# A state-space scan loop: the gates and convolution taps between the scans and the product with C

## The reference

```
xz = hidden_states @ in_proj_w.T;  x, z = split(xz)          # 1024 channels each
x = silu(causal_conv4(x) + conv_b)
dt, Bm, Cm = split(x @ x_proj_w.T)                           # 128, 16, 16
dt = softplus(dt @ dt_proj_w.T + 2 * dt_proj_b)
deltaA = exp(dt[..., None] * A);  deltaB_u = dt[..., None] * Bm[:, :, None, :] * x[..., None]
states[t] = deltaA[t] * states[t-1] + deltaB_u[t]            # 1024 channels x 16 states
y = (sum(states * Cm, -1) + x * D) * z
out = y @ out_proj_w.T
```

## Time and profile before

| | us |
|---|---|
| median of 3 runs | 3632.25 |
| lowest and highest | 3627.57, 3633.32 |
| the profiled execution | 3633.67 |
| its span, first to last instruction | 3631.7 |

### The profile page before, as it was taken

How to read it: one execution, slowest core, us unless ns; L and a number is a source line. 1 busy time by engine, 2 the same in 40 slices (tenths; PEclk the granted TensorE clock), 3 DMA queues, 4 the chain that set the end, 5 groups by cost and what they waited for, 6 DMA issues and landing times.

```text
span 3631.7 us, 30799 instructions
## 1 busy us (share of the span) xinstructions
PE 2781.9 (77%) x10802; PEld 1660.2 (46%) x10802; DVE 2316.8 (64%) x2273; ACT 1223.6 (34%) x1640; POOL 1003.3 (28%) x500
## 2 busy tenths in 40 slices
PE   5888706888598989995647768786886767779997
PEld 2333605666246779993312223232332323366665
DVE  3564365666565556663559999899899997532221
ACT  3333000000212126562244543644454332423333
POOL 0000703333102100003025555455454553011111
PEclk8888858999798999997779989998998999889998
DMA  4333911000513426663125444443453455100000
GB/s 172 101 118 64 80 20 31 0 0 0 173 58 102 163 92 248 240 223 110 36 67 151 120 121 134 130 133 112 126 143 106 127 155 178 78 1 12 12 0 23
DMA packets 230910, 359.45 MB, mean 99 GB/s; under 512 B 88432, under 2 KB 106864, under 8 KB 225168
## 3 DMA queue, kind: packets, MB, share of 16 engines
q1 hardware_dynamic: 224816, 328.67, 32.6%
q0 software_dynamic: 5120, 16.78, 1.4%
q10 hardware_dynamic: 864, 12.58, 0.8%
HBM read 304.26 MB, written 65.27 MB: 102 GB/s over the span
## 4 chain that ended last, share of the span: by engine, by line
PE 44%; DVE 27%; issue 15%; ACT 6%; DMA 3%; POOL 2%; SPq 1%; another core or an unknown queue 0%; PEld 0%; PEldq 0%; DVEq 0%; POOLq 0%; ACTq 0%
DVE arena L1093 12%; DVE arena L1100 5%; PE psum L1946 4%; PE psum L1566 3%; PE psum L1567 3%; PE psum L2050 2%; PE psum L2044 2%; DVE tmpA L1885 2%; PE psum L1329 2%; PE psum L1331 2%; PE psum L1330 2%; PE psum L2077 2%; PE psum L1554 1%; PE psum L1555 1%; PE psum L393 1%
## 5 line engine op out<-in xcount | busy, mean ns | idle before, releaser
L587 POOL TENSOR_TENSOR arena<-arena 128x1024 f32<-128x1024 f32 x256 | 630.3, 2463 | 712.6 <-DVE arena L1100 390.0
L1464 PE MATMUL psum<-arena,cst 128*128 128x512 f32 x1024 | 550.2, 668 | 291.3 <-DVE arena L1100 257.8
L1093 DVE TENSOR_TENSOR_SCAN arena<-psum,arena 128x512 f32<-128x512 f32 x512 | 595.8, 1203 | 32.3 <-POOL arena L587 22.1
L764 ACT ACTIVATE psum<-arena,negA 128x512 f32<-128x512 f32 x512 | 351.3, 690 | 646.5 <-DVE arena L1093 646.2
L1464 PEld LDWEIGHTS psum<-arena,cst 128*128 128x128 f32 x1024 | 194.1, 205 | 633.3 <-DVE arena L1100 397.1
L1647 POOL TENSOR_TENSOR arena<-arena,cst 128x1024 f32<-128x1024 f32 x96 | 200.0, 2098 | 689.3 <-DMA v_tok<-arena 353.4
L1100 DVE TENSOR_TENSOR arena<-arena 128x1024 f32<-128x1024 f32 x256 | 370.2, 1447 | 0.0
L1409 PE MATMUL psum<-arena 128*128 128x512 f32 x512 | 238.5, 612 | 36.0 <-DVE arena L1063 19.9
L1566 PE MATMUL psum<-r 128*128 128x512 f32 x512 | 209.0, 408 | 33.3 <-ACT arena L848 23.3
L1946 PE MATMUL psum<-arena 128*128 128x512 f32 x384 | 190.8, 654 | 49.2 <-DVE arena L1792 24.6
L1203 DVE TENSOR_TENSOR r<-arena,r 128x512 fp32r<-128x512 f32 x64 | 44.2, 692 | 266.9 <-ACT r L853 266.8
(11 more groups left out here) (271 smaller groups left out, 5336.8 us busy)
## 6 DMA issues: line engine op xcount, KB each, us to landing
arena<-bc_scr SPq DMA_DIRECT2D x256, 512.0 KB, 4.9
arena<-w_exp SPq DMA_DIRECT2D x23, 1408.0 KB, 6.0
arena<-in_inw SPq DMA_DIRECT2D x32, 512.0 KB, 4.6
arena<-in_gu SPq DMA_DIRECT2D x24, 512.0 KB
x_scr<-arena SPq DMA_DIRECT2D x23, 512.0 KB, 6.6
arena<-in_dn SPq DMA_DIRECT2D x23, 512.0 KB, 6.9
arena<-x_scr SPq DMA_DIRECT2D x23, 512.0 KB, 7.0
o_scr<-arena SPq DMA_DIRECT2D x23, 512.0 KB, 5.6
```

Source lines behind the costliest of these rows:

```text
L587: nc.gpsimd.tensor_tensor(dB[:, k % 4], du[:, j:j + 2], BC[:, k % RING, 0].unsqueeze(1).broadcast_to([P, 2, T]), ALU.mult).then_inc(s["db_ ...
L764: nc.scalar.activation(psum[:, 2 + t], dt[:, b % 2, j + t], ACT.Exp, scale=negA2[:, at:at + 1]).then_inc(s["da_ok"], 1)
L1093: v.tensor_tensor_scan(dB[:, k % 4, t], psum[:, 2 + t], dB[:, k % 4, t], 0.0, ALU.mult, ALU.add).then_inc(s["sc"], 1)
L1464: ins = mm(psum[:, t], ident, dB[:, k % 4, t], start=(n == 0), stop=(n == NS - 1))
```

## The change

Two calls on VectorE move from the end of a step into `scan`, between the two scans and `times_c`. The gates stay at their steps 5, 7, ... 19. The convolutions stand in step 23 + 2c instead of 21 + 2c, that is one odd step later. No instruction is added or removed, and the lists of the other four engines are the same as before.

```
--- before.py
+++ after.py
@@ -1091,6 +1091,10 @@
                 for t in range(2):
                     dve.wait_ge(s["da_ok"], 2 * k + t + 1)
                     v.tensor_tensor_scan(dB[:, k % 4, t], psum[:, 2 + t], dB[:, k % 4, t], 0.0, ALU.mult, ALU.add).then_inc(s["sc"], 1)
+                if i % 2 and b and 5 <= i < 5 + 2 * NDT:
+                    gate(b - 1, i // 2 - 2)
+                if i % 2 and b + 1 < B and 23 <= i < 23 + 2 * NDT:
+                    conv(b + 1, (i - 23) // 2)
                 if k:
                     times_c(k - 1)
 
@@ -1136,8 +1140,6 @@
                             softplus(b, 1)
                         if i == 8:
                             times_dt(b, 1)
-                        if i % 2 and 5 <= i < 5 + 2 * NDT:
-                            gate(b - 1, i // 2 - 2)
                         if i in (38, 42, 53, 56):
                             residual_tile(b - 1, (38, 42, 53, 56).index(i))
                     if b >= 2:
@@ -1146,8 +1148,6 @@
                         if i == 28:
                             scale_dve(dve, 2 * B + b - 2)
                     if nx:
-                        if i % 2 and 21 <= i < 21 + 2 * NDT:
-                            conv(nx, (i - 21) // 2)
                         if i == 58:
                             log1p_parts(nx, 0)
                         if i == 61:
```

## The result

| | before | after |
|---|---|---|
| median, us | 3628.61 (3623.58 to 3633.32, 6 runs) | 3694.06 (3689.67 to 3701.02, 6 runs) |
| ratio to before | 1 | 1.0183, 95% interval 1.0167 to 1.0199 |
| profiled execution, us | 3633.67, span 3631.7 | 3689.67, span 3686.7 |
| TensorE's mean granted clock | 0.895 | 0.889 |

What follows compares the result with a forecast made beforehand. VectorE was taken to bound the scan loop. The terms 23.4 + 23.7 + 15.1 - 1.1 - 4.6 + 5.5 = +62 us, added to 3632.25, gave 3694 us, with a range of 3657 to 3718 us.

Steps and rivals of the forecast that it cites:

- The chain: Convolution steps: late taps hold up x_tile, then sums, GpSimd, scans, next taps; a turn of 14.76 us, against 10.58 before.
- Turns: Rounds from one tile's taps to the next tile's: 12.50 us at full clock, 2.26 us more for TensorE's lower clock.
- By batch: Convolution stages, scans of step 21 to those of step 38: +23.4, +23.7 and +15.1 us in batches one to three.
- the variance matmuls: Third batch, LayerNorm matmuls ahead of x_tile(3): they fill TensorE's idle time, so that turn has no clock penalty, 12.50 us.
- the scaling: Third batch, step 28: VectorE's 3.34 + 2.29 us, which cost full time before, now lie in a turn's idle time.
- x_tile(0): Batches two and three: it waits for the last gate, now one product earlier; -1.1 us, and -4.6 in the third.
- The gates: Ahead of the product, first operation and other product meet GpSimd's end: +0.24 us each, 23 gates in the loop, +5.5.
- Costed at nothing: the loads: Row and weight loads on SP's queue: no cost; without cover, at most one landing, 4.9 us, nine times.
- a cost of the place ahead of the product: Rival set for the experiments: work ahead of the product with C delays GpSimd, sums and row loads; no chance given.
- a clock without a share: Rival set for the experiments: TensorE's lower clock adds nothing to the turns, 3694 us stays; no chance given.
- A kept clock: Rival: TensorE's clock is kept or returns at once, turns of 12.50 us; +25 us, 3658 us, 12%.
- one that stays low through all of x_tile: Rival: TensorE's clock stays low for the whole tile, +1.0 us on 17 turns; +79 us, 3711 us, 18%.

Runs made afterwards that it cites:

- a1: The kernel before with only the gates moved between the scans and the product with C; ratio to before 0.9993, loop 3.4 us shorter.
- d1: The changed kernel with x_tile(2) to x_tile(7) one step later in TensorE's list; ratio to before 0.9937, loop 20.6 us shorter.
- d3: d1 with the gates behind the product as before and x_tile(0) and x_tile(1) at steps 18 and 19; ratio to before 0.9918.
- e1: d3 with each row load issued ahead of the weight load of its step on SyncE; ratio to before 0.9906, loop 1144.3 us.
- a3: The kernel before with only the taps one odd step later, still behind the product with C; ratio to before 1.0271, loop +92.4 us.
- c1: The changed kernel with five extra matmuls, result unread, ahead of each x_tile(2) to x_tile(7) on TensorE; ratio to before 1.0097.

## Why the prediction was right

The time was forecast as 3694 and is 3694.06 us. That the two agree so closely is in part chance: the change costs 65.5 us where 62 were forecast, and the runs of before came out 3.6 us lower. By steps:

**The chain** was right in mechanism and size. Turns in the first batch: from 1956.39 to 2030.93, the ends of taps(0) and taps(5), five of them, 14.91 us each against 14.76. x_tile and the idle time ahead of it, the longest and the shortest of the 18 bursts in tiles 2 to 7:

```profile
2015.49 6.75 PE L1409 MATMUL psum<-arena 128*128 128x512 f32 x8 [5.40 <-DVE arena L1063]
...
2319.19 5.09 PE L1409 MATMUL psum<-arena 128*128 128x512 f32 x8 [5.40 <-DVE arena L1063]
```

The 18 last 5.09 to 6.75 us, mean 5.88, against 5.86 from nine bursts of other places. (A tenth, behind 28.59 us of idle time at the loop's start, had taken 6.63 and was not counted.)

**By batch**, S(21) to S(38). The first of these starts and ends, after, in the order of batches: 1944.69 and 2056.26, 2275.91 and 2388.33, 2612.75 and 2725.93. That is 111.6, 112.4 and 113.2 us against 87.11, 86.94 and 93.29: +24.5, +25.5 and +19.9, where +23.4, +23.7 and +15.1 were forecast.

**The third batch** holds the steps that failed. I had the variance matmuls keep the clock, and the scaling lie wholly in idle time. The rows say otherwise:

```profile
2633.85 3.60 PE L393 MATMUL psum<-tmpA,onesd 128*128 128x512 f32 x8
2639.41 5.40 PE L1409 MATMUL psum<-arena 128*128 128x512 f32 x8 [1.97 <-DVE arena L1063]
```

```profile
2658.39 3.35 DVE L370 RECIPROCAL dec<-dec 128x512 f32<-128x512 f32 x1
...
2661.77 2.29 DVE L375 TENSOR_TENSOR arena<-arena,dec 128x2048 f32<-128x2048 f32 x1
...
2662.51 6.04 POOL L587 TENSOR_TENSOR arena<-arena 128x1024 f32<-128x1024 f32 x2 [10.81 <-PE psum L1464]
...
2666.29 2.34 DVE L1093 TENSOR_TENSOR_SCAN arena<-psum,arena 128x512 f32<-128x512 f32 x2 [2.23 <-POOL arena L587]
```

The variance matmuls themselves ran at full speed, and after 1.97 us of idle time x_tile still took 5.40: the turn was 14.61 us, not 12.50. The trace of before had a warning of this outside, four matmuls that took 3.64 us behind 1.98 us of idle time, where others took 1.98 behind the same:

```profile
2428.50 1.98 PE L1464 MATMUL psum<-arena,cst 128*128 128x512 f32 x4 [1.98 <-DVE arena L1100]
...
2748.68 3.64 PE L1464 MATMUL psum<-arena,cst 128*128 128x512 f32 x4 [1.98 <-DVE arena L1100]
```

And GpSimd's two products took 6.04 us together instead of 4.64 beside L375; the scans began at 2666.29, 2.2 us after the scaling's end. That turn was 16.86 us, against 14.76: 1.4 us for the held GpSimd, and most of the rest for an x_tile of 6.62 us. The Trainium skill (SBUF — State Buffer, Who interferes with whom) has the two engines exclude each other there: L375 has two SBUF inputs and came first, and GpSimd's first product began 1.55 us before its end, about the 1.4 us that it lost. I had cited that rule for the gates and not applied it here.

**x_tile(0).** In the third batch S(21) waits for GpSimd no more, as forecast, and x_tile(0) took 3.67 us there. From S(38) of the batch before to S(21), the second batch took 219.65 us instead of 218.05 (+1.6) and the third 224.42 instead of 226.87 (-2.4). With a third of the gates' 5.5 us in each, forecast were +0.7 and -2.8 (the 2.96 and 1.77 us that stand beside the -4.6 make 4.73). In the second batch x_tile(0) took 1.24 us longer than the 5.21 of the earlier trace rows, though the idle time ahead of it was shorter, so the earlier gate gained nothing there:

```profile
2265.23 6.45 PE L1409 MATMUL psum<-arena 128*128 128x512 f32 x8 [4.69 <-issue]
```

**The gates** cost 0.18 us each at most, not 0.24: two in turn in the changed kernel,

```profile
2229.41 0.90 DVE L1111 SCALAR_TENSOR_TENSOR arena<-arena,cst 128x512 f32<-128x512 f32 x1
...
2237.94 0.90 DVE L1111 SCALAR_TENSOR_TENSOR arena<-arena,cst 128x512 f32<-128x512 f32 x1
```

are 8.53 us apart against 8.35 in the earlier trace rows. (The 1.43 us that the prediction calls a distance of starts are a row's length; such a product takes 1.35 from start to next start, 0.24 more than one alone.) The gate's first operation has grown from 0.74 to 0.90 us, but the two products are no longer than before, where I had one of them grow too. Over the loop this is under 4 us; in the fourth batch, S(0) to S(21) with eight gates and no x_tile, it is 0.7 (102.44 us against 101.74). In a1 it does not show against what x_tile(0) gains.

**Costed at nothing: the loads.** In the changed kernel this held; no wait for rows is in its list. In d1 and d3, where the turns are short again, the cover was gone, and e1 shows its price: 6.6 us in the convolution stages, 4.4 in the whole loop, all of it in longer products with C.

**The sum.** In the profiled loops the three stages cost 7.6 us more than forecast, and the rest of the loop came to -1.6 us where -0.2 was forecast: together +68.2, not +62. The -1.6 are the last stretch of the fourth batch, which no term of the forecast covers. In the medians the miss is 3.5 us, and the lower median of before, 3.6 us, hides it. That part is luck.

**The rivals.** a1, a3 and d1 speak against a cost of the place ahead of the product; c1 against a clock without a share. A kept clock, and one that stays low through all of x_tile, are both excluded by the bursts: 5.88 us in the mean, neither 3.60 nor 6.85. What stays open is why GpSimd comes late in d1's second and third batch and not in its first: with the row loads first (e1) the second batch is down to 78.67 us, but which of GpSimd's waits for the sums holds the third was not tried.

## What to carry to other kernels

When one engine's work moves later in a loop written in fixed steps, look through the other engines' lists for what waits for it, and for what stands behind that wait: here VectorE gained 27.7 us of its own waits for ScalarE and lost 97 (117.2 instead of 19.9) to GpSimd, because sums that had long been ready stood behind a tile that was not. Moving the waiting instruction by one step as well turned +1.8% into -0.6%, and carrying that through the loop into -0.9%. A place in the trace where the same chain already stands once prices it, hand-overs and clock included: here to 1% of the turn, 14.76 us against 14.91. And where two engines hold each other up, look at the length of their operations too, and not only at the list of waits.

## What was not expected of the hardware

TensorE's granted clock can fall after a short idle time: 17 of the 18 slow bursts came after 5.40 to 6.80 us of idle time, but one, of 5.40 us, came after 1.97 us, behind eight matmuls that had run at full speed. The granted clock was 1.00 up to 2639.4 us, 0.52 in the next 2.1 us and 0.80 in the 3.4 after them. The length of the idle time alone doesn't decide it: the two groups of four matmuls above both came after 1.98 us and behind the same row of work, one at full speed and one at about half. And extra work can make a kernel faster: 4.45 us of matmuls whose result nobody reads took 31 us (0.9%) off the changed kernel.
